# The experts' scatter adds into two arrays of sums instead of writing six rows a token

## The chip, the cores and the metric

One core of one Trainium2 chip runs the whole program. Times are microseconds of the device. A time is that of one execution of the whole kernel; where several runs are given, their median stands. The engines are called TensorE (PE in the profile, PEld for its weight loads), VectorE (DVE), ScalarE (ACT), GpSimd (POOL) and SyncE (SP, which here only issues transfers).

## The reference, cut to what matters

One block of a transformer: a modulated layer norm and attention with 16 heads over 4 x 1024 tokens of width 256, then a second modulated norm `h` and a mixture of experts. Only the second half concerns the change:

```python
# xf = h: [T, 256], T = 4 * 1024; 32 experts, 6 of them chosen for each token
combine = zeros((T, 32)).at[arange(T)[:, None], topk_idx].add(tw)   # tw: weights of the 6 chosen
def expert_step(acc, (gu, dn, c)):
    g = xf @ gu[:128].T
    u = xf @ gu[128:].T
    o = silu(g) * u @ dn.T
    return acc + c[:, None] * o
routed = scan(expert_step, 0, (experts_gate_up, experts_down, combine.T))
shared_out = (silu(xf @ shared_gate_w.T) * (xf @ shared_up_w.T)) @ shared_down_w.T
x = x + gb * (routed + shared_out)
```

Each token's routed sum has exactly six terms that are not zero. All data is float32.

## The kernel before, in words

Tokens are worked on in 8 chunks of 512 (`CH`, four tiles of 128 tokens each, `TPC`). The stages that the change touches:

**Attention and routing** (up to about 950 us). Beside the attention of the next chunk, VectorE and POOL route the tokens of the last one (`route_part`). A row of a token holds its 256 normalised values, 32 weights and 32 numbers of target rows, one for each expert (`ROW` = 256 + 2 x 32). The target of a token for an expert is 6 x token + the rank of that expert among the six (`env.tok6` + `env.rank`, by a prefix scan on VectorE, L686). POOL scatters the rows into 32 lists in DRAM, one for each expert (`scatter_chunk`, L1228). Early in the attention POOL fills spare rows behind the lists from a constant row, one transfer of 144 KB after each attention step (L1009 to L1012), and SyncE waits for them later (L898, L1298).

**Experts** (`expert_phase`). The lists are cut into 223 tiles of 128 rows (`TILES`), each of one expert. SyncE loads tile t into one of 8 buffers (`DEEP`) when tile t-8 has been used. TensorE turns it and multiplies it with the expert's weights, ScalarE and VectorE work between the products. Tile t goes through the engines in four steps, beside its neighbours. VectorE copies the tile's weights and targets out of the rows at step t (`pair`, L1732); before that it waits that the scatter of tile t-8, which read the same entries, has landed. At step t+3 VectorE multiplies the result by the weight into `y` (L1738), and POOL scatters the 128 rows of 1 KB to their target rows in DRAM with an indirect transfer (`send`, L1749 to L1754). POOL's queue goes in order: between the first sends it also scatters the last 16 parts of the last chunk's lists, one after every second tile (L1763 to L1766); those lists are needed by the last tiles only.

```python
            def send(done, n):
                pool.wait_ge(y_ok, done)
                pool.sem_inc(released, 1)
                nc.gpsimd.indirect_dma_start(
                    env.results[:, :], bass.IndirectOffsetOnAxis(ap=pair[:, n, 1:2], axis=0), y[:, n], None
                    ).then_inc(scattered[n], 16)
```

`results` has 6 rows a token, so no two rows have one target. Padding rows of a tile have targets behind these.

**Combine** (`combine_phase`). When all scatters have landed (L1820), SyncE loads the six rows of 256 tokens at a time (16 loads of 1536 KB, 4 buffers, L1824). TensorE sums three of the six by products with the identity (`add_half`, L1935), VectorE adds the other three (L1896), adds TensorE's sum (L1898), multiplies by the gate `gb` (L1900) and adds the residual `x2`, in which the shared experts' part already is (L1903); ScalarE's queue stores (L1845). The shared experts' products of three chunks (`LATE`) are done here, beside it (L1915, L1926, L1838, L1863, L1868).

Of the kernel before, what the change touches and what calls it, by code (L numbers as in the profile page):

```python
# [13 lines left out]
P = 128  # L14
# [31 lines left out]
RES_ROWS = T * TOPK + 2 * E * P  # L46
# [16 lines left out]
CONSTS = 7 + WORD  # L63
# [494 lines left out]
def route_part(dve, env, chain, c, d, of):  # L558
# [125 lines left out]
    elif d == 112:  # L684
        dve.wait_ge(env.sel_ok, c + 1)
        v.tensor_tensor_scan(env.rank[:].rearrange("p i e -> p (i e)"), env.ones[:, 0:TPC * E],  # L686
                             env.sel[:].rearrange("p i e -> p (i e)"), 0.0, ALU.mult, ALU.add)
# [13 lines left out]
    elif d == 117:  # L701
# [4 lines left out]
        v.tensor_tensor(env.rows_of(c)[:, :, TARGET:ROW].bitcast(I32), env.rank[:], bc(env.tok6[:].unsqueeze(2), TPC, E), ALU.add)  # L706
# [10 lines left out]
    elif d == 119:  # L717
        ready()
        if c < LAST:
            wait(dve, env.slot_read, c)  # L720
            largest(env.slot, E, env.places).then_inc(env.slot_ok, 1)
        else:
            then(largest(env.slot, E))
    elif d == 120 and c == LAST:
        ready()
        v.tensor_scalar(env.slot6_of(c), env.top[:, :, 0:TOPK], -1.0, None, ALU.add).then_inc(env.routed, 1)
        then(v.tensor_scalar(env.tok6[:], env.tok6[:], float(TOPK * CH), None, ALU.add))


def attention_phase(nc, env, block):  # L730
# [8 lines left out]
    with ExitStack() as ctx:  # L739
# [52 lines left out]
        def _(sp):  # L792
# [105 lines left out]
            sp.wait_ge(spare_in, 16 * (E + 1))  # L898
# [6 lines left out]
        def _(pool):  # L905
# [5 lines left out]
            g.iota(env.pad_row[:, TARGET:ROW].bitcast(I32), [[P, E]], base=T * TOPK, channel_multiplier=1  # L911
                   ).then_inc(pads_built, 1)
            g.iota(spare_to[:], [[P, E], [0, E]], base=T * TOPK + E * P, channel_multiplier=1).then_inc(pads_built, 1)
# [4 lines left out]
            g.iota(env.tok6[:], [[TOPK * P - TOPK, TPC]], base=-1, channel_multiplier=TOPK, **floats).then_inc(env.consts, 1)  # L918
# [53 lines left out]
            def weights_and_places(c):  # L972
# [4 lines left out]
                for i in range(TPC):  # L977
                    ins = g.tensor_scalar(env.rows_of(c)[:, i, TARGET:ROW].bitcast(I32), env.rank[:, i], env.tok6[:, i:i + 1],
                                          None, ALU.add)
                chain.link(ins)  # L980
                chain.link(g.tensor_scalar(env.tok6[:], env.tok6[:], float(TOPK * CH), None, ALU.add))
# [255 lines left out]
def closing_phase(nc, env, block):  # L1237
# [9 lines left out]
    with ExitStack() as ctx:  # L1247
# [49 lines left out]
        def _(sp):  # L1297
            sp.wait_ge(env.spare_in, 16 * (E + 1))  # L1298
# [239 lines left out]
def expert_phase(nc, env, block):  # L1538
# [10 lines left out]
    with ExitStack() as ctx:  # L1549
# [198 lines left out]
        def _(pool):  # L1748
            def send(done, n):  # L1749
                pool.wait_ge(y_ok, done)  # L1750
                pool.sem_inc(released, 1)
                nc.gpsimd.indirect_dma_start(  # L1752
                    env.results[:, :], bass.IndirectOffsetOnAxis(ap=pair[:, n, 1:2], axis=0), y[:, n], None
                    ).then_inc(scattered[n], 16)  # L1754

            def send_round(i, first):
                for k in range(DEEP):
                    send(DEEP * i + (k + first + 1 - DEEP), (first + k) % DEEP)
# [20 lines left out]
def combine_phase(nc, env, block):  # L1779
# [3 lines left out]
    BUFS = 4  # L1783
    SUMS = 2
# [4 lines left out]
    with ExitStack() as ctx:  # L1789
        def sb(name, shape, dt=F32):  # L1790
            return ctx.enter_context(nc.sbuf_tensor(name, shape, dt))

        most = BUFS * WIDE * TOPK * D
        six = env.wide[:, 0:most].rearrange("p (n i j d) -> p n i j d", n=BUFS, i=WIDE, j=TOPK)
        result = env.wide[:, most:most + BUFS * WIDE * D].rearrange("p (n i d) -> p n i d", n=BUFS, i=WIDE)
        half = TOPK // 2
        added, halves_done, halves_read, ch = (env.sem("co_" + n) for n in ("added", "halves_done", "halves_read", "chain"))
        psS = ctx.enter_context(nc.psum_tensor("co_psS", [P, SUMS, WIDE, D], F32))
        six_in, stored = ([env.sem(f"co_{n}{u}") for u in range(BUFS)] for n in ("six_in", "stored"))
# [10 lines left out]
        results = env.results[0:T * TOPK].rearrange("(c i p j) d -> c p i j d", i=WIDE, p=P, j=TOPK)  # L1810
# [7 lines left out]
        def _(sp):  # L1818
            for u, landed in enumerate(env.landed):
                sp.wait_ge(landed, 16 * ((TILES - u + len(env.landed) - 1) // len(env.landed)))  # L1820
            for n, c in enumerate(order):
                u = n % BUFS
                wait(sp, added, n - BUFS + 1)
                sp.dma_start(six[:, u], results[c]).then_inc(six_in[u], 16)  # L1824

        @block.scalar
        def _(act):
# [11 lines left out]

            for k, m in ((0, 0), (0, 1), (1, 0)):  # L1840
                late_silu(k, m)
            for n, c in enumerate(order):
# [3 lines left out]
                if n in (0, 1, 2):  # L1846
                    late_silu(*((1, 1), (2, 0), (2, 1))[n])
            for u in range(BUFS):
                act.wait_ge(stored[u], 16 * ((NCH - u + BUFS - 1) // BUFS))

        @block.vector
        def _(dve):
# [17 lines left out]
            def beside(n):  # L1870
                if n == 1:
                    add_late(0)
                    multiply_late(1, 0)
                elif n == 2:
                    multiply_late(1, 1)
                elif n == 4:
                    add_late(1)
                    multiply_late(2, 0)
                elif n == 5:
                    multiply_late(2, 1)  # L1880
                elif n == 7:
# [7 lines left out]
            for n, c in enumerate(order):  # L1889
                u, b = n % BUFS, c * WIDE * P // S  # L1890
                beside(n)
                if c == late[0]:
                    dve.wait_ge(y_read, len(LATE))
# [235 lines left out]
```

## Time and the profile before

| | |
|---|---|
| median of 3 runs | 1425.0 us (1424.52 to 1428.65) |
| the profiled execution, its own time | 1430.49 us |
| its span, first to last instruction | 1428.7 us |
| TensorE busy | 1359.2 us (95%) |
| VectorE busy | 1129.7 us (79%) |
| POOL busy | 606.7 us (42%) |
| the experts' scatters, first to last begin | 962.6 to 1335.6 us |
| the last stage | 1338.1 to 1428.7 us |
| bytes moved in the whole span | 243.55 MB |

A span is measured from the first to the last instruction of the profiled execution; the time of an execution is a little longer. The busy share is an average over stages with different limits: each stage is to be read by itself.

### The profile page before, as it was taken

Reading aid. Unit: us, or ns where it says so; the run is one execution under the profiler, and the core shown is the slowest. Engines: PE = TensorE matmul, PEld = TensorE weight load, DVE = VectorE, ACT = ScalarE, POOL = GpSimd, SP = SyncE. Lnnn points to the kernel's source line nnn. Section 1 sums busy time; section 2 is a strip of 40 time slices with the busy share of each in tenths; the row PEclk is TensorE's granted clock in tenths of the full one; section 3 lists DMA queues with packets and bytes.
Section 4 is the critical chain, followed back from the end, with each engine's and each line's share of the span. In section 5 each row is a group of like instructions: output and inputs, shape, how many; then the busy total and the mean of one; then the engine's idle time right before and its main releaser. Section 6 shows DMA issues by size and latency. Waiting matters only on the chain.

```text
span 1428.7 us, 30863 instructions
## 1 busy us (share of the span) xinstructions
PE 1359.2 (95%) x8207; PEld 677.6 (47%) x8208; DVE 1129.7 (79%) x2815; ACT 754.5 (53%) x1155; POOL 606.7 (42%) x782
## 2 busy tenths in 40 slices
PE   7997999999999999999999999989999999999996
PEld 3552223332333323333333233558788888887552
DVE  7886999999999999999999992656566666665477
ACT  3772577667666767676667677113333333333100
POOL 4000113233744725546346366327755555555200
PEclk9997799999999999999999999999999999999998
DMA  6887355534346435454465346837766656555788
GB/s 213 273 266 201 102 165 134 112 91 106 99 127 166 103 101 140 124 135 101 112 162 146 80 134 198 257 124 237 226 202 203 203 168 189 180 173 173 270 304 317
DMA packets 216960, 243.55 MB, mean 170 GB/s; under 512 B 93949, under 2 KB 181501, under 8 KB 216738
## 3 DMA queue, kind: packets, MB, share of 16 engines
q1 hardware_dynamic: 189330, 166.42, 42.8%
q0 software_dynamic: 21776, 68.07, 13.4%
q10 hardware_dynamic: 5760, 7.87, 1.7%
q8 instruction: 51, 0.84, 0.2%
q14 instruction: 43, 0.35, 0.1%
HBM read 133.98 MB, written 108.28 MB: 170 GB/s over the span
## 4 chain that ended last, share of the span: by engine, by line
PE 68%; DVE 14%; DMA 5%; issue 2%; SPq 1%; ACT 1%; POOL 0%; DVEq 0%; POOLq 0%
PE psO L1171 14%; PE ex_psGU L1670 13%; PE psE L1158 13%; PE psM L1148 9%; DVE piece_max L1046 9%; PE ex_psY L1685 6%; PE ex_psX L1661 3%; PE psM L505 2%; PE co_psS L1935 2%; PE ex_psA L1679 2%; DMA wide<-results 1%; DMA results<-vals_inv,places 1%; PE psGU L1486 1%; PE late_psGU L1915 1%; PE psM L524 1%
## 5 line engine op out<-in xcount | busy, mean ns | idle before, releaser
L1046 DVE TENSOR_REDUCE piece_max<-psM 128x1 f32<-128x512 f32 x1024 | 642.2, 681 | 28.6 <-PE psM L1148 25.3
L1112 ACT ACTIVATE wide<-psE 128x1024 f32<-128x1024 f32 x512 | 497.1, 1021 | 208.4 <-PE psE L1158 206.2
L1148 PE MATMUL psM<-wide 48*128 48x512 bf16 x1024 | 324.5, 396 | 20.4 <-DVE piece_max L1046 12.0
L1158 PE MATMUL psE<-wide 49*128 49x512 bf16 (+1 forms) x2048 | 331.0, 382 | 2.4 <-DMA wide<-maxima 2.4
L1752 POOL DMA_INDIRECT results<-vals_inv,places x223 | 213.9, 959 | 155.9 <-DVE vals_inv L1738 89.9
L1171 PE MATMUL psO<-wide 128*32 128x512 f32 x2048 | 275.4, 610 | 0.6 <-ACT wide L1112 0.6
L1148 PEld LDWEIGHTS psM<-wide 48*128 48x128 bf16 x1024 | 78.2, 93 | 348.4 <-DVE piece_max L1046 275.8
L1670 PE MATMUL ex_psGU<-wide,ex_xT 128*128 x892 | 233.0, 384 | 0.6 <-ACT ex_xT L1703 0.6
L1158 PEld LDWEIGHTS psE<-wide 49*128 49x128 bf16 (+1 forms) x2048 | 117.9, 95 | 94.0 <-issue 10.4
L1670 PEld LDWEIGHTS ex_psGU<-wide,ex_xT 128*128 128x128 f32 x892 | 153.1, 192 | 15.6 <-issue 2.9
L1703 ACT ACTIVATE ex_xT<-ex_psX 128x256 f32<-128x256 f32 x223 | 85.6, 384 | 123.7 <-PE ex_psX L1661 122.5
L1685 PE MATMUL ex_psY<-wide,ex_actT 128*128 x446 | 136.1, 387 | 1.0 <-DVE ex_actT L1720 0.7
L1232 POOL DMA_INDIRECT lists<-last_rows,slot x96 | 93.5, 974 | 102.1 <-PE psO L1171 59.2
L1232 POOL DMA_INDIRECT lists<-rows,slot x96 | 93.9, 978 | 77.6 <-PE psO L1171 59.4
L1708 ACT ACTIVATE ex_silu<-ex_psGU 128x128 f32<-128x128 f32 x223 | 61.9, 278 | 113.8 <-PE ex_psGU L1670 113.4
L1720 DVE COPY ex_actT<-ex_psA 128x128 f32<-128x128 f32 x223 | 64.1, 287 | 62.7 <-PE ex_psA L1679 62.0
L1738 DVE TENSOR_SCALAR vals_inv<-ex_psY,places 128x256 f32<-128x256 f32 x223 | 107.6, 483 | 1.1 <-PE ex_psY L1685 1.1
L1685 PEld LDWEIGHTS ex_psY<-wide,ex_actT 128*128 128x128 f32 x446 | 67.2, 190 | 22.5 <-issue 7.8
L1171 PEld LDWEIGHTS psO<-wide 128*32 128x32 f32 x2048 | 40.4, 108 | 69.3 <-issue 64.8
L1725 DVE TENSOR_TENSOR ex_act<-ex_psGU,ex_silu 128x128 f32<-128x128 f32 x223 | 63.1, 283 | 2.8 <-ACT ex_silu L1708 2.8
L420 PE MATMUL psQK<-hT,wqkv 128*128 128x512 f32 x128 | 58.7, 613 | 6.6 <-ACT hT L365 6.6
L1679 PE MATMUL ex_psA<-ident,ex_act 128*128 128x128 f32 x223 | 61.1, 274 | 1.3 <-DVE ex_act L1725 1.1
(280 smaller groups left out, 1271.8 us busy)
## 6 DMA issues: line engine op xcount, KB each, us to landing
wide<-qk_parts SPq DMA_DIRECT2D x384, 64.0 KB
wide<-results SPq DMA_DIRECT2D x16, 1536.0 KB, 8.6
rows<-lists SPq DMA_DIRECT2D x112, 160.0 KB
h2Ts<-lists SPq DMA_DIRECT2D x111, 160.0 KB
qk_parts<-parts SPq DMA_DIRECT2D x32, 384.0 KB, 3.0
xin<-in_x_dram SPq DMA_DIRECT2D x16, 512.0 KB, 4.0
v_values<-vst SPq DMA_DIRECT2D x32, 256.0 KB, 3.6
wide<-v_values SPq DMA_DIRECT2D x16, 512.0 KB
```

The costliest lines, as they stand in the source:

```text
L1046: v.tensor_reduce(piece_max[:, qh, (x * PAIRS + h) * KT // QH + qt, kh:kh + 1], bank_of("piece", PIECES * group + n), AX.X, ALU.max, negat ...
L1112: nc.scalar.activation(probs[:, step % 2, 2 * pair:2 * pair + 2], psE[:, pair], ACT.Exp, scale=HD ** -0.5).then_inc(exp_ok, 1)
L1148: nc.tensor.matmul(bank_of(*user), qa[g][rows, h, qt * P:(qt + 1) * P], ka[g][rows, h, kh * 512:(kh + 1) * 512], start=True, stop=True).th ...
L1158: mm = nc.tensor.matmul(psE[:, pair, x], k[g][part, pair, kt * P:(kt + 1) * P], q[g][part, pair, qh * 512:(qh + 1) * 512], start=(q is qa) ...
L1171: mm = nc.tensor.matmul(psO[32 * h:32 * h + 32], va[g][:, kt, 32 * h:32 * h + 32], probs[:, s % 2, 2 * pair + x], start=(kt == 0), stop=(k ...
L1232: nc.gpsimd.indirect_dma_start(env.lists[:, :], bass.IndirectOffsetOnAxis(ap=env.slot6_of(c)[:, i, j:j + 1], axis=0), env.rows_of(c)[:, i, ...
L1670: mm = nc.tensor.matmul(psGU[:, n, 0:2 * INTER], xT[:, n, k * P:(k + 1) * P], gu_w[:, bass.ds(e, 1), k].rearrange("p o n -> p (o n)"), sta ...
L1679: nc.tensor.transpose(psA[:, u % 2, 0:P], act_e[:, u % 2], env.ident[:]).then_inc(a_done, 1)
L1685: nc.tensor.matmul(psY[:, n, 0:D], actT[:, n], down_w[:, bass.ds(e, 1)].rearrange("p o n -> p (o n)"), start=True, stop=True).then_inc(y_d ...
L1703: nc.scalar.activation(xT[:, u % 2], psX[:, u % 2, 0:D], ACT.Copy).then_inc(x_ok, 1)
L1738: nc.vector.tensor_scalar(y[:, n], psY[:, (u + 1) % 2, 0:D], pair[:, n, 0:1].bitcast(F32), None, ALU.mult).then_inc(y_ok, 1)
L1752: nc.gpsimd.indirect_dma_start(env.results[:, :], bass.IndirectOffsetOnAxis(ap=pair[:, n, 1:2], axis=0), y[:, n], None).then_inc(scattered ...
```

## The change

Instead of `results` with six rows a token there are two arrays of sums in DRAM, each with one row a token (and 128 rows for padding). The scatter of tile t adds its 128 rows to the rows of array t mod 2. Two tiles may hold the same token, so before tile t is sent, POOL waits that tile t-2, which adds into the same array, has landed. The arrays are zeroed early in the attention by POOL, two further transfers of 128 KB behind each spare-row transfer. Targets become the token's number; the prefix scan that ranked the experts goes. In the last stage two rows a token are loaded (two loads of 256 KB for 256 tokens, 6 buffers instead of 4), POOL adds the two, VectorE multiplies by the gate and adds the residual; TensorE's identity products and VectorE's other additions go. The late shared products are spread over other steps of the loop.

```diff
-RES_ROWS = T * TOPK + 2 * E * P
+SUM_ROWS = T + P
+SETS = 2
...
     elif d == 112:
         dve.wait_ge(env.sel_ok, c + 1)
-        v.tensor_tensor_scan(env.rank[:].rearrange("p i e -> p (i e)"), env.ones[:, 0:TPC * E],
-                             env.sel[:].rearrange("p i e -> p (i e)"), 0.0, ALU.mult, ALU.add)
...
-            sp.wait_ge(spare_in, 16 * (E + 1))
+            sp.wait_ge(spare_in, 16 * (SETS + 1) * (E + 1))
...
+            def clear_sums(a, first, end):
+                pool.dma_start(env.sums_d[a].rearrange("(k p) d -> p k d", p=P)[:, first:end],
+                               env.pad_row[:, 0:D].unsqueeze(1).to_broadcast([P, end - first, D])).then_inc(spare_in, 16)
+
             for k in range(E):
                 pool.wait_ge(summed, k + 1)
                 pool.dma_start(spare[:, k, 0:TARGET], env.pad_row[:, 0:TARGET]).then_inc(spare_in, 16)
+                for a in range(SETS):
+                    clear_sums(a, k, k + 1)
+            for a in range(SETS):
+                clear_sums(a, E, SUM_ROWS // P)
...
-            def send(done, n):
+            def send(done, n, landed):
                 pool.wait_ge(y_ok, done)
+                wait(pool, scattered[(n - SETS) % DEEP], landed)
                 pool.sem_inc(released, 1)
                 nc.gpsimd.indirect_dma_start(
-                    env.results[:, :], bass.IndirectOffsetOnAxis(ap=pair[:, n, 1:2], axis=0), y[:, n], None
-                    ).then_inc(scattered[n], 16)
+                    env.sums_d[n % SETS][:, :], bass.IndirectOffsetOnAxis(ap=pair[:, n, 1:2], axis=0), y[:, n], None,
+                    compute_op=ALU.add).then_inc(scattered[n], 16)
...
+            pool.wait_ge(env.spare_in, 16 * (SETS + 1) * (E + 1))
...
-                send(t + 1, t % DEEP)
+                send(t + 1, t % DEEP, 16 * ((t - SETS) // DEEP + 1))
...
-    BUFS = 4
+    BUFS = 6
...
-                sp.dma_start(six[:, u], results[c]).then_inc(six_in[u], 16)
+                for a in range(SETS):
+                    sp.dma_start(sums[:, u, :, a], results[a][c]).then_inc(sums_in[u], 16)
...
+        @block.gpsimd
+        def _(pool):
+            for n in range(NCH):
+                u = n % BUFS
+                pool.wait_ge(sums_in[u], 16 * SETS * (n // BUFS + 1))
+                nc.gpsimd.tensor_tensor(sums[:, u, :, 0], sums[:, u, :, 0], sums[:, u, :, 1], ALU.add
+                                        ).then_inc(paired, 1)
...
-                dve.wait_ge(six_in[u], 16 * (n // BUFS + 1))
-                for j in range(half + 1, TOPK):
-                    chain.link(v.tensor_tensor(six[:, u, :, half], six[:, u, :, half], six[:, u, :, j], ALU.add))
-                dve.wait_ge(halves_done, n + 1)
-                v.tensor_tensor(six[:, u, :, half], six[:, u, :, half], psS[:, n % SUMS], ALU.add).then_inc(halves_read, 1)
-                dve.wait_ge(halves_read, n + 1)
-                chain.link(v.tensor_tensor(six[:, u, :, half], six[:, u, :, half],
+                if c in late:
+                    dve.wait_ge(y_read, late.index(c) // (TPC // WIDE) + 1)
+                dve.wait_ge(paired, n + 1)
+                chain.link(v.tensor_tensor(sums[:, u, :, 0], sums[:, u, :, 0],
                                            env.modb[:, b, 3].unsqueeze(1).to_broadcast([P, WIDE, D]), ALU.mult))
                 wait(dve, stored[u], 16 * (n // BUFS))
-                v.tensor_tensor(result[:, u], six[:, u, :, half], env.x2[:, WIDE * c:WIDE * (c + 1)], ALU.add
+                v.tensor_tensor(result[:, u], sums[:, u, :, 0], env.x2[:, WIDE * c:WIDE * (c + 1)], ALU.add
                                 ).then_inc(added, 1)
```

## Rows read from the trace of the kernel before

**Rows 1.** Windows: engines' busy time (instructions), granted clock, DMA share, GB/s.
```profile
160.00:240.00 80.00, 78.42 (x622) 23.32 (x620) 78.15 (x133) 61.49 (x66) 16.55 (x31) 1.00 0.51 153
1020.00:1328.00 308.00, 307.27 (x1655) 252.28 (x1655) 189.38 (x736) 121.78 (x368) 179.91 (x189) 1.00 0.62 186
1338.00:1429.00 91.00, 74.46 (x182) 35.06 (x180) 60.91 (x88) 2.98 (x5) 0.00 (x0) 0.93 0.85 323
1390.00:1400.00 10.00, 7.66 (x17) 2.69 (x15) 9.62 (x15) 0.00 (x0) 0.00 (x0) 1.00 0.98 339
```

**Rows 2.** The scatter's lines (L1752, L1751): ns min/median/max, first and last start, waiters.
```profile
L1752 POOL DMA_INDIRECT results<-vals_inv,places x223: 954/959/1070, 962.6 to 1335.6; - x112
...
  DVE places L1732: 8.0, 8
...
L1751 POOLq EVENT_SEMAPHORE  x223: 17/17/17, 961.8 to 1334.1; - x112
```

**Rows 3.** DMA issues: count, KB each, median us from issue to landing.
```profile
wide<-results SPq DMA_DIRECT2D x16, 1536.0 KB, 8.6
...
xin<-in_x_dram SPq DMA_DIRECT2D x16, 512.0 KB, 4.0
...
out_dram<-wide ACTq DMA_DIRECT2D x16, 256.0 KB, 7.6
...
cT<-in_cT_dram SPq DMA_DIRECT2D x1, 4.0 KB, 3.1
```

**Rows 4.** Groups by line in the last stage, 1338 to 1429.
```profile
L1935 PE MATMUL co_psS<-wide,ident 128*128 128x512 f32 x96 | 49.1, 658 | 10.5 <-DMA wide<-results 10.1 <-DVE wide L1898 0.4
...
L1915 PE MATMUL late_psGU<-h2Ts,wsg 128*128 128x512 f32 x32 | 14.5, 592 | 0.0
L1900 DVE TENSOR_TENSOR wide<-wide,modb 128x512 f32<-128x512 f32 x16 | 11.1, 692 | 0.6
...
L1868 DVE TENSOR_TENSOR x<-late_psX,x 128x1024 f32<-128x1024 f32 x3 | 3.7, 1222 | 1.2 <-PE late_psX L1926 1.2
L1926 PE MATMUL late_psX<-wo,act_s 128*128 128x256 f32 x16 | 3.6, 379 | 0.0
...
L1915 PE MATMUL late_psGU<-xin,wsg 128*128 128x512 f32 x6 | 2.7, 592 | 0.0
```

**Rows 5.** Chain of waits around the last scatters, 1329 to 1345.
```profile
1329.51 0.02 POOLq L1751
...
1330.28 0.23 POOL results L1752
...
1335.64 2.42 DMA results<-vals_inv,places
1338.06 0.02 issue
1338.08 0.03 SPq L1820
```

**Rows 6.** Chain of waits at the very end: start, us, what.
```profile
1425.32 0.69 DVE wide L1903
```

**Rows 7.** POOL's and VectorE's lines beside the change: spare rows, values, prefix scan.
```profile
L1011 POOL DMA_DIRECT2D lists<-pad_row x32: 540/540/569, 159.8 to 240.1; - x32
...
  PE psO L1171: 94.7, 32
...
265.13 2.35 POOL L935 TENSOR_TENSOR vals_inv<-vals_inv 128x1024 f32<-128x1024 f32 x1 [18.42 <-DMA vals_inv<-inverse_sums]
...
L686 DVE TENSOR_TENSOR_SCAN rank<-ones,sel x8: 408/412/424, 320.3 to 931.8; 128x128 f32<-128x128 bf16 x8
```

**Rows 8.** Chain of waits, 955 to 1045: start, us, what.
```profile
999.30 2.68 DMA results<-vals_inv,places
1003.10 2.69 DMA results<-vals_inv,places
1006.89 3.43 DMA results<-vals_inv,places
...
1018.27 3.34 DMA results<-vals_inv,places
```

**Rows 9.** Timeline of POOL at the start of the scatters.
```profile
963.86 0.96 POOL L1232 DMA_INDIRECT lists<-last_rows,slot  x1 [0.30 <-issue]
965.13 0.96 POOL L1752 DMA_INDIRECT results<-vals_inv,places  x1 [0.30 <-issue]
```

More of the change, by code:

```diff
@@ L62 @@
 ROUNDS = 3
-CONSTS = 7 + WORD
+CONSTS = 8 + WORD
 VALS_LOADS = 2 * KC
@@ L705, in route_part @@
                                in1=bc(env.wrec[:].unsqueeze(2), TPC, E), op0=ALU.mult, op1=ALU.mult)
-        v.tensor_tensor(env.rows_of(c)[:, :, TARGET:ROW].bitcast(I32), env.rank[:], bc(env.tok6[:].unsqueeze(2), TPC, E), ALU.add)
+        v.tensor_tensor(env.rows_of(c)[:, :, TARGET:ROW].bitcast(I32), env.no_offset[:], bc(env.token[:].unsqueeze(2), TPC, E), ALU.add)
     elif d == 116:
@@ L726, in route_part @@
         v.tensor_scalar(env.slot6_of(c), env.top[:, :, 0:TOPK], -1.0, None, ALU.add).then_inc(env.routed, 1)
-        then(v.tensor_scalar(env.tok6[:], env.tok6[:], float(TOPK * CH), None, ALU.add))
+        then(v.tensor_scalar(env.token[:], env.token[:], float(CH), None, ALU.add))
 def attention_phase(nc, env, block):
@@ L977, in weights_and_places @@
                 for i in range(TPC):
-                    ins = g.tensor_scalar(env.rows_of(c)[:, i, TARGET:ROW].bitcast(I32), env.rank[:, i], env.tok6[:, i:i + 1],
+                    ins = g.tensor_scalar(env.rows_of(c)[:, i, TARGET:ROW].bitcast(I32), env.no_offset[:, i], env.token[:, i:i + 1],
                                           None, ALU.add)
                 chain.link(ins)
-                chain.link(g.tensor_scalar(env.tok6[:], env.tok6[:], float(TOPK * CH), None, ALU.add))
+                chain.link(g.tensor_scalar(env.token[:], env.token[:], float(CH), None, ALU.add))
                 pool.wait_ge(env.slot_ok, c + 1)
@@ L1791, in sb @@
             return ctx.enter_context(nc.sbuf_tensor(name, shape, dt))
-        most = BUFS * WIDE * TOPK * D
-        six = env.wide[:, 0:most].rearrange("p (n i j d) -> p n i j d", n=BUFS, i=WIDE, j=TOPK)
+        most = BUFS * WIDE * SETS * D
+        sums = env.wide[:, 0:most].rearrange("p (n i j d) -> p n i j d", n=BUFS, i=WIDE, j=SETS)
         result = env.wide[:, most:most + BUFS * WIDE * D].rearrange("p (n i d) -> p n i d", n=BUFS, i=WIDE)
[L1796 to L1799, printed above, removed]
+        added, paired, ch = (env.sem("co_" + n) for n in ("added", "paired", "chain"))
+        sums_in, stored = ([env.sem(f"co_{n}{u}") for u in range(BUFS)] for n in ("sums_in", "stored"))
         (gu_done, silu_ok, a_ok, y_done, y_read, wsd_ok) = (env.sem("late_" + n) for n in (
@@ L1809, in combine_phase @@
         turned_in = lambda k: ((env.late_in, 16), (env.h2T_in[0], 16 * 3), (env.h2T_in[1], 16 * 2))[k]
-        results = env.results[0:T * TOPK].rearrange("(c i p j) d -> c p i j d", i=WIDE, p=P, j=TOPK)
+        results = [env.sums_d[a][0:T].rearrange("(c i p) d -> c p i d", i=WIDE, p=P) for a in range(SETS)]
         out = env.out.rearrange("(c i p) d -> c p i d", i=WIDE, p=P)
@@ L1928, in late_out @@
                 mm.then_inc(y_done, 1)
-            def add_half(n):
-                u = n % BUFS
-                pe.wait_ge(six_in[u], 16 * (n // BUFS + 1))
-                wait(pe, halves_read, n - SUMS + 1)
-                for j in range(half):
-                    mm = nc.tensor.matmul(psS[:, n % SUMS], env.ident[:], six[:, u, :, j], start=(j == 0), stop=(j == half - 1))
-                mm.then_inc(halves_done, 1)
             pe.wait_ge(env.x_ok, TILES)
@@ L1992, in declare @@
     env.table_d = dram("tile_table", (2 * P, 2), I32)
-    env.results = dram("results", (RES_ROWS, D), F32)
+    env.sums_d = [dram(f"sums{a}", (SUM_ROWS, D), F32) for a in range(SETS)]
 def declare_projection(nc, env, ctx):
@@ L2030, in declare_routing @@
     env.stats = sb("stats2", [P, TPC, 6])
[L2031 to L2032 removed]
+    env.mean, env.diff, env.var, env.minus_half, env.rstd, env.newton, env.wsum, env.wrec, env.token = (
+        sb(n, [P, TPC]) for n in ("mean2", "diff2", "var2", "minus_half", "rstd2", "newton2", "wsum", "wrec", "token"))
     env.guess = sb("guess", [P, TPC], I32)
[L2034 removed]
+    env.sc, env.sfc, env.chosen, env.no_offset = (sb(n, [P, TPC, E]) for n in ("sc", "sfc", "chosen", "no_offset"))
     env.slot = env.sfc
```

40 lines of the change are left out of this document (15 added, 25 removed).

## Prediction

> **What bounds the kernel now.** I read the span by stages first, then the chain of waits through each stage that the change touches. The reader is to see two stages with different limits. In the experts' stage (window 1020 to 1328 [rows 1]) TensorE is busy 307.27 of 308 us at full clock, while the DMA engines are 62% busy and POOL's 189 records take 180 us. POOL sends 223 scatters between 962.6 and 1335.6 [rows 2], 373.0 us over 222 intervals, 1.68 us each. Nobody waits for a scatter except VectorE, eight times, 8.0 us in all [rows 2], because a buffer comes back only after eight tiles. So the latency of a scatter is hidden today behind seven others. In the last stage (window 1338 to 1429 [rows 1]) the DMA engines are busy 0.85 of it and 0.98 in the ten us from 1390; the load of six rows a token costs 8.6 us from issue to landing [rows 3], and the chain of waits alternates between these loads and the identity products that sum three of the six rows (49.1 us of TensorE [rows 4]). This stage is bound by the bytes of the results.
>
> **What the last stage gives back.** It lasts from the last landing, 1335.64 + 2.42 = 1338.06 [rows 5], to 1428.7: 90.6 us. It moves 16 loads of 1536 KB and 16 stores of 256 KB [rows 3], 29.4 MB, 325 GB/s. The new one moves 16 x 512 KB and the same stores, 12.6 MB: 38.7 us at that rate. Rows of 1 KB instead of 6 KB may go a little slower; I leave that to the range. Ahead of it stands the first load (512 KB of x took 4.0 us [rows 3]), of which some 1.5 us is already bytes in the sum; behind it POOL's addition of 128x512, half of the 2.35 us that 128x1024 takes [rows 7], 1.2 us, VectorE's two operations (0.69 us each [rows 4]), and the last store, 2.7 us from VectorE's last end at 1426.0 to the span's [rows 6], of which 0.8 us is bytes in the sum. I take 38.7 + 2.5 + 1.2 + 1.4 + 1.9 = 45.7 us. The engines fit beneath: VectorE 16 x 2 x 0.72 = 23 us plus three additions of 1.22 and four products of 0.69, 29.4 us; POOL 16 x 1.2 = 19 us; TensorE keeps only the late shared products (14.5 + 2.7 + 3 x 3.6 = 28 us in this window [rows 4]), which may start before the last scatters have landed. Saved: 90.6 - 45.7 = 45 us. If rows of 1 KB move at only two thirds of the rate, it is 19 us less, 26 us; if VectorE sets the pace, 29.4 + 7 us, it is 54 us.
>
> **The wait in the experts' stage.** Before the changed code sends tile t, POOL waits until tile t-2 has landed, and the transfer reads and adds in DRAM instead of only writing. POOL serves its queue in order, so tile t+1 stands behind that wait, and behind it, in the first 32 tiles, one of the 16 list scatters after every second tile. VectorE waits for the landing of t-8, SyncE for VectorE's copy, so the whole stage soon runs at the pace of the scatters. For one array the cycle is
> C = (POOL's wait ends to the scatter's record begins) + L (record to landing) + (landing to the end of the wait), and a tile takes C/2, since two arrays alternate.
> The first term is in the chain of waits [rows 5]: the wait ends at 1329.51, the scatter's record begins at 1330.28, 0.77 us. The last term is small: SyncE's queue ends its wait 0.02 to 0.05 us after the last landing at 1338.06 [rows 5]; I put 0.06 us for POOL's. L for a plain scatter is on the chain wherever somebody waited for one: 2.68, 2.69, 3.43 and 3.34 us [rows 8], and 2.42 us for the last one, when the queues are quiet [rows 5]; the mean of the five is 2.9. Already a plain scatter would give C = 0.77 + 2.9 + 0.06 = 3.73 and 1.87 us a tile instead of 1.68. That is the heart of this forecast: the chain of landings replaces TensorE as the limit even if the addition is free.
>
> What the addition adds to L, no row shows. From below it is nothing (the row in DRAM is read beside the row in SBUF), or what 128 KB more cost: a load of 512 KB takes 4.0 us and one of 4 KB 3.1 us [rows 3], 0.23 us for 128 KB. From above it is a whole small read of DRAM ahead of the write, 3.1 us [rows 3]. A load's 3.1 us contains an issue and a signal that the scatter has already paid; the scatter has to pay the way to DRAM and back once more, twice the bytes through the adder, and one more descriptor a row to generate. I take 1.0 us, a third of a whole read: L = 3.9, C = 4.73, 2.37 us a tile.
>
> The first wait ends at 961.8 [rows 2]; the last of 223 tiles, number 222, starts after 111 cycles and lands a cycle later: 961.8 + 112 x 4.73 = 1491.6. Before it was 1338.1: 153.5 us more. POOL's own pace does not add to this: records follow each other after 1.26 us [rows 9], so two scatters and one list are 3.8 us in a cycle of 4.73.
>
> Here two statements of the Trainium skill stand against each other. Its page "DMA: Bandwidth & Descriptors" (the fit for a DMA issued by GpSimd, above its table of where the 2 us go) gives 2.0 us plus bytes over 436 GB/s; for 128 KB that is 2.3 us, near the quiet row's 2.42, and by it twice the bytes would add only 0.3 us (an estimate from that page), which is the faster rival below. The same page, "Latency and other measured facts", puts the access to HBM at 0.2 us on average and 2 us under high load, and calls it the main part of the fixed cost; by it one more access would add between 0.2 and 2 us. No row here tells the two apart.
>
> **What costs nothing or nearly.** The two arrays must be zeroed: 66 more transfers of 128 KB on POOL's queue in the attention's first steps, two behind each spare-list transfer. One such takes 0.54 us of POOL, one is issued a step, and POOL waits 94.7 us for the steps meanwhile [rows 7], some 2.6 us a step (32 between 159.8 and 240.1); three with gaps of 0.3 us just fill that. POOL's next duty, the product of the values, waits 18.42 us for its data [rows 7]. The DMA engines are 0.51 busy there [rows 1]; the extra 8.7 MB over 80 us are 108 GB/s beside 153. If that delays the maxima, a few us; not in the sum. If POOL were late, its cover is those 18 us. The prefix scan on VectorE goes, 8 x 0.41 = 3.3 us [rows 7], in a stage where VectorE is near its limit (78.15 of 80 us [rows 1]); I take 2 us of it. POOL's constants (one memset more, other integers) change nothing. Waiting for the zeroing at the head of the scatters and in SyncE's queue is past by 700 us.
>
> **Sum.** 153.5 - 45 - 2 = +106.5 us. The profiled execution took 1430.5 us (span 1428.7); the median of the runs is 1425.0. I put the difference on the median: 1531 us. It does not rest on details of the last stage: each 0.1 us of L is 11.2 us. The break-even is 112 C = 376.3 + 47, C = 3.78, L = 2.95 us.
>
> **The rivals.**
> A, faster: an adding scatter is hardly longer than the quiet plain one, because most of L is a fixed round trip, and the slower pace thins out the traffic that stretched 2.42 to 3.43. L = 2.42 + 0.23 = 2.65, C = 3.48: 961.8 + 389.8 = 1351.6, +13.5 - 47 = -33.5, 1391 us. For it: the quiet row, and the width between quiet and crowded rows. Against: tiles still overlap with 160 KB row loads, and a read of DRAM is free in none of the rows. It decides below L = 2.91. 0.17 for all of that side. The fit named above is this rival's: by it 1390 us or so.
> B, no difference: L between 2.91 and 2.99, the plain mean with a free addition, 1421 to 1429 us. 0.04.
> C, the likeliest: L of 3.0 to 4.9, at the 1531 us of the sum, with its own range of 1464 to 1621 (L = 3.3 to 4.7). 0.69.
> D, the reads and writes of the row follow one another and each pays a full trip, L = 2.9 + 3.1 = 6.0, C = 6.83: 961.8 + 765 = 1727, +342, 1767 us. 0.10 for L above 4.9.
> E, POOL becomes the limit: two reads for a write may double POOL's 0.96 us for a scatter. Then a tile takes no less than 1.92 + 0.3 = 2.22 us whatever L is, 222 x 2.22 = 493 us, last landing near 1459, +73 us, 1498 us. It decides only if L is below 3.6; it lies in C's range and takes the place of A there. It holds part of C's chance.
> A clock that falls because TensorE is busy 70% of the time would not show: at half clock a tile's products take at most 3.3 us, and TensorE has five tiles of lead, since VectorE waits for the landing of t-8 only. The window from 1390, 77% busy, kept the full clock [rows 1].
>
> **Chances.** About 0.3% either way is what a measurement of this kernel tells from no change. Faster 0.17, same 0.04, slower 0.79. For the range I leave out the lower half of A (below 1400, 0.09) and D (above 1640, 0.10).
>
> **What the profile will show.** If right: POOL's scatters begin in pairs every 4.7 us, and the releaser of POOL's idle time is the landing in the arrays of sums, no longer VectorE's product; TensorE about 70% busy in that stage; the last landing near 1490; the last stage about 45 us with DMA as its bound; nothing changed before 950. Wrong, if POOL's record of a scatter is much above 1 us (E), if a tile still takes about 1.7 us (A), or if the attention's stage is longer, which would be the zeroing.

## The result and the profile after

The changed kernel takes 1556.5 us in the median of 4 runs (1554.67 to 1559.08), the one before 1426.8 us: a ratio of 1.09, 95% interval 1.0855 to 1.0946. The forecast was 1531 us, within 1400 to 1640. The profiled execution took 1555.6 us, its span is 1553.9 us, 125.2 us more than before.

The scatter's line in the changed kernel, the lines that answer to [rows 2]:
```profile
L1761 POOL DMA_INDIRECT sums<-vals_inv,places x223: 1550/1550/1618, 967.5 to 1501.1; - x112
...
  DVE places L1740: 207.2, 152
  POOL sums L1761: 33.5, 29
...
DMA to landing us min/median/max: 3.6/3.9/6.4
```
There are three things to see. The scatters last 533.6 us instead of 373.0. A landing, for which only VectorE waited, eight times and 8.0 us, is now waited for 152 times by VectorE (207.2 us) and by POOL itself. And POOL's record of one scatter has grown from 0.96 to 1.55 us. The landing takes 3.9 us in the median, which is the L of the forecast. The profile names the landing for 29 of POOL's waits only; 140.5 us of POOL's idle time before the scatters it books as "issue", that is to no releaser. So this line alone does not show that POOL waits for landings; the experiments below do.

The chain of waits of the changed kernel from 1200 to 1230, start and us (x: pieces merged):
```profile
1198.23 6.20 DMA sums<-vals_inv,places x2
1204.43 1.29 issue
...
1205.95 10.62 DMA sums<-vals_inv,places x4
...
1217.33 6.19 DMA sums<-vals_inv,places x2
1223.52 1.27 issue
```
TensorE, which set this stage's pace before, is not on it. What alternates are landings and POOL's start of the next scatter. POOL's timeline in the same stretch shows the pairs (start, us, and in brackets the idle time before):
```profile
1205.95 1.55 POOL L1761 DMA_INDIRECT sums<-vals_inv,places  x1 [1.52 <-issue]
1207.80 1.55 POOL L1761 DMA_INDIRECT sums<-vals_inv,places  x1 [0.30 <-issue]
1210.57 1.55 POOL L1761 DMA_INDIRECT sums<-vals_inv,places  x1 [1.22 <-issue]
1212.43 1.55 POOL L1761 DMA_INDIRECT sums<-vals_inv,places  x1 [0.30 <-issue]
1215.47 1.55 POOL L1761 DMA_INDIRECT sums<-vals_inv,places  x1 [1.49 <-issue]
```
The second of a pair follows after POOL's own 1.86 us (1.55 us and a gap of 0.30), the next pair 4.6 to 4.9 us after the first. From 1039.9 to 1478.0 there are 186 scatters, 2.368 us a tile, a cycle of 4.74 us; the forecast had 4.73.

The windows that answer to [rows 1], the experts' stage and the last one:
```profile
160.00:240.00 80.00, 76.74 (x594) 22.34 (x590) 75.02 (x128) 59.43 (x63) 47.32 (x89) 0.98 0.79 247
...
1020.00:1328.00 308.00, 256.32 (x1151) 176.24 (x1150) 127.53 (x511) 84.91 (x256) 204.25 (x136) 0.99 0.77 137
...
1504.00:1554.00 50.00, 21.45 (x54) 12.09 (x52) 37.95 (x39) 1.79 (x3) 23.12 (x16) 0.71 0.77 253
```
In the experts' stage TensorE completes 1151 products in 308 us instead of 1655. The DMA engines are busier than before (0.77 against 0.62) while they move less (137 GB/s against 186): an adding transfer occupies them longer for a byte. TensorE is busy 0.83 of the stage, where the forecast had about 70%; its granted clock is 0.99.

The last scatter and the start of the last stage (chain of waits), which answer to [rows 5]:
```profile
1501.12 3.74 DMA sums<-vals_inv,places
1504.88 0.03 SPq L1827
...
1506.47 4.24 DMA wide<-sums
```
The last landing is at 1504.9 and the last stage takes 1553.9 - 1504.9 = 49.0 us, 41.6 less than before. Span against span: the first scatter begins 4.9 us later, the scatters to the last landing take 161.9 us more, the last stage 41.6 less: +125.2 us.

### The profile page after: what moved, and what is told of

Same layout as the page of the kernel before. It is cut to its first block, busy times and chain, and to the rows that moved or that the text cites. A ratio compares the mean times of both kernels' runs of the same rounds, so it can differ in the third digit from the quotient of the medians.

```text
span 1553.9 us, 30734 instructions
## 1 busy us (share of the span) xinstructions
PE 1388.1 (89%) x8111; PEld 662.9 (43%) x8112; DVE 1099.9 (71%) x2759; ACT 755.7 (49%) x1155; POOL 797.9 (51%) x865
## 4 chain that ended last, share of the span: by engine, by line
PE 36%; DMA 35%; DVE 12%; issue 5%; SPq 1%; POOL 1%; ACT 1%; POOLq 0%; DVEq 0%
DMA sums<-vals_inv,places 31%; PE psO L1179 12%; PE psE L1166 11%; DVE piece_max L1054 8%; PE psM L1156 8%; PE psM L506 2%; DMA maxima<-neg_max_t 1%; DMA wide<-maxima 1%; PE psM L525 1%; DVE wide L1914 1%; DMA o_sums<-o_sb 1%; POOL sums L1761 1%; SPq L796 1%; PE psGU L1494 1%; ACT wide L1120 1%
## 5 line engine op out<-in xcount | busy, mean ns | idle before, releaser
L1761 POOL DMA_INDIRECT sums<-vals_inv,places x223 | 346.4, 1554 | 186.6 <-issue 140.5
L1678 PE MATMUL ex_psGU<-wide,ex_xT 128*128 x892 | 237.3, 389 | 1.1 <-ACT ex_xT L1711 0.6
L1693 PE MATMUL ex_psY<-wide,ex_actT 128*128 x446 | 151.3, 421 | 3.9 <-DVE ex_actT L1728 0.6
L1687 PE MATMUL ex_psA<-ident,ex_act 128*128 128x128 f32 x223 | 70.3, 315 | 77.0 <-DVE ex_act L1733 74.8
L1740 DVE COPY places<-h2Ts 128x2 int32 x111 | 19.5, 176 | 149.8 <-DMA sums<-vals_inv,places 109.9
L1740 DVE COPY places<-rows 128x2 int32 x112 | 19.9, 177 | 141.7 <-DMA sums<-vals_inv,places 97.2
L1687 PEld LDWEIGHTS ex_psA<-ident,ex_act 128*128 128x128 f32 x223 | 31.2, 140 | 144.7 <-DVE ex_act L1733 135.0
```

The lines of the kernel that those rows point to most:

```text
L1678: mm = nc.tensor.matmul(psGU[:, n, 0:2 * INTER], xT[:, n, k * P:(k + 1) * P], gu_w[:, bass.ds(e, 1), k].rearrange("p o n -> p (o n)"), sta ...
L1687: nc.tensor.transpose(psA[:, u % 2, 0:P], act_e[:, u % 2], env.ident[:]).then_inc(a_done, 1)
L1693: nc.tensor.matmul(psY[:, n, 0:D], actT[:, n], down_w[:, bass.ds(e, 1)].rearrange("p o n -> p (o n)"), start=True, stop=True).then_inc(y_d ...
L1761: nc.gpsimd.indirect_dma_start(env.sums_d[n % SETS][:, :], bass.IndirectOffsetOnAxis(ap=pair[:, n, 1:2], axis=0), y[:, n], None, compute_o ...
```

## Experiments

Every comparison is with the kernel before, run on the same chip; ratios carry their 95% interval. Line numbers are each kernel's own. "Tile" is the mean distance between scatters in the steady stretch, from about the last list scatters on, worked out from the first and last start and the count of the scatter's line there.

**The wait alone**, in the kernel before.
```diff
-            def send(done, n):
+            def send(done, n, landed):
                 pool.wait_ge(y_ok, done)
+                wait(pool, scattered[(n - 2) % DEEP], landed)
```


> The kernel before, with plain scatters into six rows a token, and one thing more: before tile t is sent, POOL waits that the scatter of tile t-2 has landed. Nothing is left out. If the chain of landings is the cause: C = 0.77 + 2.9 + 0.06 = 3.73 us, 1.87 us a tile instead of 1.68, 222 intervals 414 us instead of 373, the rest unchanged: about 1467 us. If the cause is the longer record on POOL or the traffic of the additions, and the wait is hidden, the time stays at 1427 us.

1467.5 us, ratio 1.0258 (1.0229 to 1.0288). The scatter's line:
```profile
L1753 POOL DMA_INDIRECT results<-vals_inv,places x223: 954/958/967, 961.5 to 1374.5; - x112
...
  DVE places L1732: 128.8, 147
  POOL results L1753: 60.6, 49
```
413.0 us over 222 intervals, 1.86 us; the last stage stays at 90.9 us. The wait costs 40 us of the scatters' stretch (38 us of the whole) although each scatter is as short as before. That it would be hidden is refuted.

**The wait and everything else, without the addition**, in the changed kernel.
```diff
-                    env.sums_d[n % SETS][:, :], bass.IndirectOffsetOnAxis(ap=pair[:, n, 1:2], axis=0), y[:, n], None,
-                    compute_op=ALU.add).then_inc(scattered[n], 16)
+                    env.sums_d[n % SETS][:, :], bass.IndirectOffsetOnAxis(ap=pair[:, n, 1:2], axis=0), y[:, n], None).then_inc(scattered[n], 16)
```


> The changed kernel with the wait on tile t-2, but the scatter writes its rows instead of adding them, so the sums of the six experts are left out. If the wait is the mechanism and the addition lengthens the landing by 1 us: L falls from 3.9 to 2.9, C from 4.8 to 3.73, the scatters take 414 us instead of 534, and the whole 1436 us. If the addition costs nothing and another part of the change makes the scatters slow, it stays at 1556 us. If POOL's longer record (1.55 instead of 0.96 us) alone is the cause, the tile falls back to 1.68 us and the whole to 1394 us.

1428.2 us, ratio 0.9992 (0.9975 to 1.0009).
```profile
L1761 POOL DMA_INDIRECT sums<-vals_inv,places x223: 954/958/967, 969.2 to 1379.2; - x112
...
DMA to landing us min/median/max: 2.4/2.7/3.5
```
POOL's record is 0.96 us again and the landing 2.7 us, so 1.2 us of L and 0.6 us of POOL's record belong to the addition. The whole came out 8 us below the 1436 us expected, because the plain landing is 2.7 and not 2.9 us: the tile is 1.80 us. The wait's loss and the last stage's gain cancel here; all of the changed kernel's 9% hangs on the addition inside the wait.

**Four arrays, so that the wait is for tile t-4.** `READ` is 2.
```diff
-SETS = 2
+SETS = 4
+SET_OF = (0, 1, 2, 3, 0, 1, 2, 3)
+BACK = (4,) * 8
...
-                wait(pool, scattered[(n - SETS) % DEEP], landed)
+                wait(pool, scattered[(n - BACK[n]) % DEEP], landed)
...
-                for a in range(SETS):
+                for a in range(READ):
```


> The changed kernel with four arrays of sums instead of two, so that POOL waits on tile t-4; the last stage still reads two of them (what the other two hold is left out of the sums), and four arrays are zeroed. If the chain of landings is the cause, C/4 = 1.2 us no longer binds and POOL does: 1.55 + 0.30 = 1.85 us a tile, 411 us of scatters, the whole about 1440 us (a few us for the further zeroing within). If the additions' traffic in DRAM is the cause, whatever the wait, the tile stays at 2.4 us and the whole at 1556 us. If POOL's records overlap with its waiting and TensorE is the limit again, 1.68 us a tile and 1400 us.

1465.2 us, ratio 1.0245 (1.0209 to 1.0282), and POOL's timeline is what was expected of it:
```profile
1205.95 1.55 POOL L1763 DMA_INDIRECT sums<-vals_inv,places  x1 [0.30 <-DMA sums<-vals_inv,places]
1207.81 1.55 POOL L1763 DMA_INDIRECT sums<-vals_inv,places  x1 [0.30 <-DMA sums<-vals_inv,places]
1209.66 1.55 POOL L1763 DMA_INDIRECT sums<-vals_inv,places  x1 [0.30 <-issue]
```
Scatter after scatter at 1.86 us: the chain of landings is gone and POOL's own record is the limit. The additions are all still there, so their traffic alone does not set 2.37 us a tile. The total missed my 1440 us because I forgot the 16 list scatters in POOL's now full queue (20.6 us; 978.6 to 1412.4 is 433.8 us, and 222 x 1.86 + 20.6 = 433.5) and because four arrays to zero delay the first scatter to 978.6.

**The zeroing alone**, in the kernel before.
```diff
                 pool.dma_start(spare[:, k, 0:TARGET], env.pad_row[:, 0:TARGET]).then_inc(spare_in, 16)
+                for a in range(2):
+                    clear_sums(a, k, k + 1)
```


> The kernel before with the 66 zeroing transfers of 128 KB added to POOL's queue in the attention (into arrays that nobody reads) and the waits on them. Nothing is left out. If the zeroing is what moved the first scatter from 962.6 to 967.5 us: 1427 + 5 = 1432 us, with the loss between 160 and 250 us. If it is hidden as the sum had it, 1427 us, and the 5 us come from elsewhere.

1435.1 us, ratio 1.0039 (1.0021 to 1.0056), about 6 us. The first scatter begins at 968.4. Who waited for whom from 160 to 260 (us, times, longest):
```profile
PEld psE L1166 <- DMA wide<-maxima: 4.1, 3, 2.6
PE psE L1166 <- DMA wide<-maxima: 3.2, 3, 2.3
```
Before, the same two rows are 1.7 and 1.2 us. The two rows are one wait seen twice, by the weight load and by the product behind it, so one of them counts: 4.1 instead of 1.7 us. POOL is not late (it still waits for each step); the small transfers of the maxima, on TensorE's path, are waited for longer while the zeroing runs, and that is 2.4 of the 6 us. The rest has no single row, but it is lost in the same stretch: from 160 to 250 TensorE completes 660 products instead of 702, worth 5.4 us, at a granted clock of 0.97 instead of 1.00. With four arrays the two rows grow to 8.3 and 7.4 us.

**The last stage alone**: the kernel before up to the last scatter, then the changed last stage.
```diff
-        results = env.results[0:T * TOPK].rearrange("(c i p j) d -> c p i j d", i=WIDE, p=P, j=TOPK)
+        results = [env.results[a * T:(a + 1) * T].rearrange("(c i p) d -> c p i d", i=WIDE, p=P) for a in range(SETS)]
```


> The kernel before up to the last scatter (plain writes, six rows a token, no wait, no zeroing) with the changed kernel's last stage, which loads two rows a token; the other four are left out of the sums. If the last stage's gain is its own, bytes and additions: from 90.6 to about 49 us, the whole 1427 - 42 = 1385 us. If the gain needs the slower scatters (late products done while they land): nearer 55 us and 1391 us.

1388.8 us, ratio 0.9729 (0.9704 to 0.9754): 39.5 us gained, with scatters between 961.5 and 1334.3 as before. The gain is the last stage's own.

**One array.**
```diff
-SETS = 2
+SETS = 1
+SET_OF = (0,) * 8
+BACK = (1,) * 8
```


> One array of sums: tile t waits for the landing of tile t-1; only one array is zeroed. The last stage reads the one array twice, so the routed sums are taken double. If a tile takes C over the number of arrays: C = 4.81 us a tile, 223 x 4.81 = 1073 us, from 965 to 2038, with the last stage 2087 us. If part of C (the start of the scatter, 0.77, or POOL's record) were paid once for both arrays in the changed kernel and not twice here, clearly less than 4.81 us a tile: 4.0 us and 1900 us.

2041.1 us in its one run. From 1063.6 to 1899.0 there are 182 scatters, 4.615 us a tile. So a tile does take C over the number of arrays, with C 4.6 us here and 4.74 with two, and TensorE, whose granted clock from 1020 to 1900 falls to 0.75, still keeps up. The expected 4.81 us had been taken from all 222 intervals, with the slower first ones in it.

**Three arrays, whole computation.** As with four, with `SET_OF = (0, 1, 2, 0, 1, 2, 0, 1)`, `BACK = (2, 2, 5, 3, 3, 3, 3, 3)`, and three identity products on TensorE to add three rows.

> Three arrays of sums, used in the order 0 1 2 0 1 2 0 1 by eight tiles, each waiting for its own array; three arrays are zeroed; the last stage loads three rows a token and TensorE adds them. Nothing is left out. Chain of landings: 3 C for 8 tiles, 1.8 us a tile, below POOL's own 1.86, so POOL binds as with four arrays: 223 x 1.86 + 20 for the lists = 435 us, last landing about 1410, last stage 16.8 MB at 325 GB/s and 7 us around it, 59 us: about 1470 us. If each wait still cost in proportion to its distance: 1.8 to 2.1 us a tile and up to 1510 us.

1525.0 us, ratio 1.0663 (1.0638 to 1.0687). Two misses. The tile is 2.10 us: two of every eight tiles wait for the tile two before them, and that wait adds to POOL's own pace along the queue, where I had taken the larger of two means. The starts show it: seven gaps of 1.86 us, then one of 3.6 us (from 1200.85 to 1204.46), 16.6 us for eight tiles. And the last stage takes 68.1 us, since TensorE's identity products set it, as the next experiment shows. It is still slower than the kernel before.

**TensorE adds the two rows.**
```diff
-                nc.gpsimd.tensor_tensor(sums[:, u, :, 0], sums[:, u, :, 0], sums[:, u, :, 1], ALU.add
+                for j in range(SETS):
+                    mm = nc.tensor.matmul(psS[:, n % 2], env.ident[:], sums[:, u, :, j], start=(j == 0), stop=(j == SETS - 1))
```


> The changed kernel, where TensorE adds the two rows by two identity products into PSUM in place of POOL's addition. Nothing is left out. In the changed kernel VectorE's two operations took 1.02 and 1.05 us in the mean against 0.69 before, and POOL's addition 1.45 instead of 1.2. If VectorE and POOL hinder each other: VectorE's operations fall back to 0.69 us, 16 x 0.69 = 11 us less of VectorE, some of it on the path, the last stage 44 to 46 us instead of 49 and the whole about 1552 us. If the loads and stores bind the last stage, no change: 1556 us.

1559.7 us, ratio 1.0926 (1.0903 to 1.0949). Groups by line in its last stage, 1501 to 1555:
```profile
L1943 PE MATMUL co_psS<-wide,ident 128*128 128x512 f32 x64 | 30.5, 624 | 2.6 <-DMA wide<-sums 2.6
...
L1911 DVE TENSOR_TENSOR wide<-wide,x 128x512 f32<-128x512 f32 x16 | 11.1, 692 | 0.5
L1907 DVE TENSOR_TENSOR wide<-co_psS,modb 128x512 f32<-128x512 f32 x16 | 11.0, 687 | 30.5 <-PE co_psS L1943 30.5
```
VectorE's operations did fall back to 0.69 us, but VectorE waits 30.5 us for TensorE, and the stage takes 54.6 us: TensorE is the limit, so this run could not tell what the contention costs the stage.

**VectorE adds the two rows; and, in another kernel, the late products left out.** The first edit is the one's, the second the other's (the same products go on TensorE and ScalarE).
```diff
+                dve.wait_ge(sums_in[u], 16 * SETS * (n // BUFS + 1))
+                chain.link(v.tensor_tensor(sums[:, u, :, 0], sums[:, u, :, 0], sums[:, u, :, 1], ALU.add))
...
-                beside(n)
-                if c in late:
-                    dve.wait_ge(y_read, late.index(c) // (TPC // WIDE) + 1)
```


> The changed kernel with VectorE itself adding the two rows, three operations in a row for 256 tokens, and POOL idle in the last stage. Nothing is left out. If VectorE and POOL hinder each other, so that POOL's help is worth little: VectorE's operations back at 0.69 us, 16 x 3 x 0.72 + 6.4 = 41 us of VectorE and some 7 us around it, 48 us for the last stage, as now, the whole 1556 us. If POOL's addition really takes work off the path: 16 x 0.7 = 11 us longer, 60 us and 1567 us.

> The changed kernel without the late shared products: the shared experts' part of three chunks is left out, and with it all of TensorE's and ScalarE's arithmetic and seven of VectorE's operations in the last stage. If the order of these products, on which VectorE waits in its loop, sets the last stage (49 us): it falls to about 43 us, loads, stores and latencies, and the whole to about 1550 us. If bytes, or VectorE and POOL hindering each other, set it: 48 to 49 us and 1556 us.

VectorE alone: 1552.7 us, ratio 1.0876 (1.0847 to 1.0904). No late products: 1553.9 us, ratio 1.0875 (1.0842 to 1.0908). Neither can be told from the changed kernel by its time; the profiles can. From the last landing to the end it is 1504.0 to 1549.3, 45.3 us, and 1508.0 to 1552.8, 44.8 us, against 49.0. VectorE's and POOL's rows in the last stage, first of the changed kernel, from 1504 to 1554:
```profile
L1865 POOL TENSOR_TENSOR wide<-wide 128x512 f32<-128x512 f32 x16 | 23.1, 1454 | 20.0 <-DMA wide<-sums 19.8
L1917 DVE TENSOR_TENSOR wide<-wide,x 128x512 f32<-128x512 f32 x16 | 16.8, 1051 | 0.6
L1914 DVE TENSOR_TENSOR wide<-wide,modb 128x512 f32<-128x512 f32 x16 | 16.4, 1023 | 13.2 <-POOL wide L1865 13.1
```
then of the kernel where VectorE adds, from 1500 to 1553:
```profile
L1907 DVE TENSOR_TENSOR wide<-wide,modb 128x512 f32<-128x512 f32 x16 | 11.1, 692 | 0.6
L1910 DVE TENSOR_TENSOR wide<-wide,x 128x512 f32<-128x512 f32 x16 | 11.1, 692 | 0.5
L1906 DVE TENSOR_TENSOR wide<-wide 128x512 f32<-128x512 f32 x16 | 10.9, 683 | 14.0 <-DMA wide<-sums 14.0
```
48 operations by VectorE alone take 33.1 us; 32 beside POOL take 33.2. POOL's help takes nothing off VectorE.

The windows of the two kernels, where VectorE adds (1500 to 1550) and without the late products (1503 to 1553), say what sets the pace (VectorE's busy time is the third, 37.64 and 35.07 us):
```profile
1500.00:1550.00 50.00, 19.30 (x56) 10.51 (x54) 37.64 (x55) 1.79 (x3) 1.55 (x1) 0.77 0.79 257
1503.00:1553.00 50.00, 0.00 (x0) 0.00 (x0) 35.07 (x32) 0.00 (x0) 25.41 (x18) 0.50 0.80 257
```
Where VectorE adds, its 37.64 us lie between its first operation at 1507.7 and its last end at 1546.4, 38.7 us, and it waits once only, for the first load (14.0 us). Without the late products it is 35.07 of 36.8 us (1513.1 to 1549.9). In the changed kernel it is some 37.7 of 41.3 us (1509.8 to 1551.0). VectorE sets the pace of this stage in all three.

**Half the width, half the rows.**
```diff
-    env.sums_d = [dram(f"sums{a}", (SUM_ROWS, D), F32) for a in range(SETS)]
+    env.sums_d = [dram(f"sums{a}", (SUM_ROWS, D // 2), F32) for a in range(SETS)]
...
-                    env.sums_d[n % SETS][:, :], bass.IndirectOffsetOnAxis(ap=pair[:, n, 1:2], axis=0), y[:, n], None,
+                    env.sums_d[n % SETS][:, :], bass.IndirectOffsetOnAxis(ap=pair[:, n, 1:2], axis=0), y[:, n, 0:D // 2], None,
```
```diff
-                    env.sums_d[n % SETS][:, :], bass.IndirectOffsetOnAxis(ap=pair[:, n, 1:2], axis=0), y[:, n], None,
+                    env.sums_d[n % SETS][:, :], bass.IndirectOffsetOnAxis(ap=pair[0:P // 2, n, 1:2], axis=0), y[0:P // 2, n], None,
```


> The changed kernel with rows of 128 values in the arrays of sums: each adding scatter still has 128 rows, but half the bytes (the other half of the sums is left out; the last stage loads half as much). If the addition's extra time is bytes through the DMA engines, L falls from 3.9 to about 3.4 us and the tile from 2.4 to 2.15 us; POOL's record stays at 1.55 us. If it is made of work for each row (POOL's 1.55 us for 128 rows) and a round trip, L stays within 0.2 us of 3.9 and the tile at 2.3 us or more.

> The changed kernel with the first 64 of the 128 rows of every tile added, in full width (the other 64 rows are left out of the sums). If the extra time is work for each row, POOL's record falls from 1.55 to about 0.9 us, L from 3.9 to about 3.3 us and the tile to 2.1 us. If it is a round trip that does not depend on rows, L stays at 3.7 us or more and the tile at 2.3 us.

| scatter of a tile | POOL's record | landing, median | tile, steady | total |
|---|---|---|---|---|
| plain, 128 rows of 1 KB, wait on t-2 | 0.96 us | 2.7 us | 1.80 us | 1428.2 us |
| adding, 128 rows of 1 KB | 1.55 us | 3.9 us | 2.37 us | 1556.5 us |
| adding, 128 rows of 0.5 KB | 1.55 us | 3.3 us | 2.12 us | 1504.0 us |
| adding, 64 rows of 1 KB | 1.40 us | 3.2 us | 2.03 us | 1481.2 us |

The last two totals are single runs. Halving the bytes in either way takes 0.6 to 0.7 us off the landing, about half of the 1.2 us that the addition adds. That points to bytes for most of it, but a plain scatter of half the size, which would say how much of the 0.6 us the plain one has too, was not run.

The packet counts show how the two kinds travel, first the changed kernel, then the run without the addition:
```profile
DMA packets 245887, 235.41 MB, mean 151 GB/s; under 512 B 95261, under 2 KB 219549, under 8 KB 245666
DMA packets 224480, 235.41 MB, mean 165 GB/s; under 512 B 95262, under 2 KB 191006, under 8 KB 224259
```
That is 28543 packets more under 2 KB and 7136 fewer larger ones, for the same bytes: for each of 223 scatters 128 packets of one row instead of 32 of four rows. Half the width has as many packets as the full one, half the rows half as many, and their landings differ by 0.1 us.

POOL's work for each row is small, since half the rows cost 1.40 instead of 1.55 us. The expectation that half the rows would give a record of 0.9 us was wrong. The half-width run tells one thing more: its last stage loads half the bytes (128 KB a load, landing in 2.7 us) and lasts from 1453.1 to 1502.3, 49.2 us, as long as the changed kernel's. Bytes of the loads do not bind that stage any more.

## Why the prediction was right, step by step

**The wait makes a chain of landings.** Right and shown: alone it costs 40 us (forecast 1.87 us a tile, measured 1.86); with one array a tile takes the whole cycle, with four the chain is gone.

**C = 0.77 + L + 0.06.** Right: 4.73 forecast, 4.74 measured. The same sum, with each run's own landing, comes within 0.12 us of the others: 4.63 against 4.615 with one array, 3.53 against 3.60 without the addition, 4.13 against 4.24 with half the width, 4.03 against 4.06 with half the rows. Within L two terms were off against each other. The plain landing in this pattern is 2.7 us, not the 2.9 us that [rows 8] and the last scatter averaged to, and the addition costs 1.2 us, not 1.0. That L came out at 3.9 us is partly luck.

**What the addition costs.** The lower bound, 0.23 us for 128 KB by the plain loads, was a fifth of the true price, and the upper one of 3.1 us was far off too. If the 1.2 us are mostly bytes, as the two half runs suggest, they go at about a fifth of the loads' marginal rate. The fit of the Trainium skill ("DMA: Bandwidth & Descriptors", the fit for a DMA issued by GpSimd) gives 2.6 us for twice the bytes, an estimate from that page. The trace's 3.9 us for an adding scatter disagrees, and decides.

**The last landing at 1491.6.** Measured 1504.9, 13.3 us later. 4.9 of it is the first scatter's later start, and 1.1 the slightly longer cycle (112 x 0.01). The rest, 7.3 us, is the mis-sized term: I had let two scatters and one list pass in 3.8 us under a cycle of 4.73, from POOL's records of before. With records of 1.55 us they need 2 x 1.86 + 1.29 = 5.0 us, and POOL binds as long as there are lists: the first 16 pairs of the changed kernel take 82.5 us (967.5 to 1050.0), 5.15 us each, 6.6 us more than at 4.74. Rival E had the right mechanism, a longer record, with too large a price (1.92); it binds only in this stretch, and with four arrays.

**The zeroing at nothing.** Wrong by about 5 us. POOL's queue had room for it, as argued; the cost came at least in part by the other way named, the maxima, and was left out of the sum. In a single profile this is blurred: five others with the same zeroing have their first scatter between 963.1 and 969.5, so that the 6 us rest on the 12 runs of the zeroing alone.

**The prefix scan's 2 us** cannot be seen in any run; it lies within the spread of the first scatter's start.

**The last stage at 45.7 us.** Measured 49.0: near in the number, wrong in the mechanism, so the nearness is luck. It was to be bound by bytes at 325 GB/s, but with half the load bytes it takes the same time, and the window shows 253 GB/s where before there were 323. What binds it is VectorE, which the forecast had put beneath the bytes with 29.4 us and named as the case of a shorter stage. The stage is 4.9 us up to VectorE's first operation, 41.3 us of VectorE, of which it is busy some 37.7, and 2.9 us for the last store. The term that was too small is VectorE's two operations at 0.72 us each: they took 1.02 and 1.05 us, because POOL and VectorE hinder each other. Without POOL's addition VectorE has a third operation instead, and the stage takes 45.3 us; without the late products 44.8 us.

**The sum.** +106.5 us forecast, +125.2 us in span: 13.3 by the last landing, 3.3 by the last stage, 2 by the scan make up the 18.7 us between. Rivals A, B and D are refuted by the landing of 3.9 us. Of the versions run here none that computes everything beats the kernel before: two arrays 1.09, three 1.066. With four, the last landing is at 1416, 78 us later than before, and the last stage, even with two rows a token, gave back 42.

## What to carry to other kernels

Before a wait is put between two transfers, write down the cycle that it closes: wait's end to issue, issue to landing, landing to the wait's end, divided by how many such chains run beside each other; compare it with the pace of the stage, even if the transfer itself costs nothing more. A latency that was hidden behind eight buffers becomes the pace behind two. And a change that saves bytes in one place by adding in DRAM at another has to be priced for each transfer that adds: here 42 us saved stood against 0.7 us on each of 223 tiles.

## What the runs showed of the hardware

An indirect scatter of 128 rows of 1 KB from SBUF to DRAM occupies POOL 0.96 us and lands 2.7 us after its record begins; with an addition in the transfer it is 1.55 us and 3.9 us. For 64 rows it is 1.40 us and 3.2 us, for rows of 512 bytes 1.55 us and 3.3 us.

POOL and VectorE share more than I had expected. In the changed kernel's last stage POOL did six additions of 128x512 in a row, in 9.85 us, while VectorE did the same kind of work:
```profile
1508.47 1.26 POOL L1865 TENSOR_TENSOR wide<-wide 128x512 f32<-128x512 f32 x1 [5.80 <-DMA wide<-sums]
...
1512.66 9.85 POOL L1865 TENSOR_TENSOR wide<-wide 128x512 f32<-128x512 f32 x6 [0.35 <-DMA wide<-sums]
...
1514.62 0.68 DVE L1880 TENSOR_TENSOR h2T<-late_psGU,h2T 128x512 f32<-128x512 f32 x1
...
1516.41 1.64 DVE L1917 TENSOR_TENSOR wide<-wide,x 128x512 f32<-128x512 f32 x1
1517.97 1.75 DVE L1914 TENSOR_TENSOR wide<-wide,modb 128x512 f32<-128x512 f32 x1
...
1525.40 0.69 DVE L1917 TENSOR_TENSOR wide<-wide,x 128x512 f32<-128x512 f32 x1
```
VectorE's operation takes 0.69 us by itself and 1.64 to 1.75 us beside POOL's, whose own goes from 1.26 to 1.64 us. Strictly in turn a pair would take 1.95 us, side by side 1.26; they come nearer to taking turns. The Trainium skill has this ("SBUF — State Buffer", Who interferes with whom): a VectorE instruction with two inputs in SBUF contends with a GpSimd instruction that reads SBUF. The trace agrees, with these numbers. VectorE's product with one input in PSUM took 0.68 us at 1514.62, amid the same six additions, no longer than by itself.

TensorE's clock, granted at 0.99 in the experts' stage, was 0.71 in the mean from 1504 to 1554. TensorE had no product from 1506.2 to 1515.4, and from 1515 to 1525 the clock was 0.50, which is 1.2 of 2.4 GHz; 16 of the late products took 6.7 us from 1522.1 on instead of 3.6.
